# Attention and feed-forward layer: value matmuls taken one head group late, value and output projections in each other's place

## What is computed

```python
qkv = hidden_states @ Wqkv
q, k, v = jnp.split(qkv, 3, axis=-1)
q = rmsnorm(q, q_norm_w)
k = rmsnorm(k, k_norm_w)
# 16 heads of 32 columns
q = rope(q, cos, sin)
k = rope(k, cos, sin)
mask = (q_idx >= k_idx) & (q_idx - k_idx <= WINDOW - 1)   # WINDOW = 256
scores = jnp.einsum('bqhd,bkhd->bhqk', q, k) * scale
scores = jnp.where(mask[None, None, :, :], scores, jnp.float32(-jnp.inf))
probs = jax.nn.softmax(scores, axis=-1)
o = jnp.einsum('bhqk,bkhd->bqhd', probs, v).reshape(b, s, h)
return o @ Wo
# and around it: x = layernorm(x + attention(x))
```

## The kernel before

| Group | projection | turned |
|---|---|---|
| 0 | queries of s + 1 | `spread`, the reciprocal sums of block s - 1 |
| 1 | keys of s + 1 | `x1` of block s - 2 |
| 2 | output of s - 1 | the rotated queries of s + 1 |
| 3 | values of s + 1 | the rotated keys of s + 1 |

## Time and profile before

### The profile page before, as it was taken

One profiled execution on the slowest core, in us unless ns is written; L12 is line 12 of the kernel. 1 busy time (PEld: TensorE's weight loads), 2 busy tenths in 40 slices (PEclk: granted clock), 3 DMA queues, 4 the chain that ended last, 5 costly groups with the idle time before them and its releaser, 6 DMA issues.

```text
span 1096.1 us, 19793 instructions
## 1 busy us (share of the span) xinstructions
PE 1039.7 (95%) x7116; PEld 855.9 (78%) x7116; DVE 766.6 (70%) x1165; ACT 639.4 (58%) x1301; POOL 446.9 (41%) x548
## 2 busy tenths in 40 slices
PE   4899999999999977999999999999999999999995
PEld 3677777777777754887888888888888888887884
DVE  4887777787877763874766677777676777674573
ACT  4566666666666654334566666666766666664353
POOL 4677887777788730001122222222222222221271
PEclk8899999999999986899999999999999999999998
DMA  5111111111111103356798999999999999995562
GB/s 203 32 50 33 32 32 31 32 47 47 31 31 32 31 30 109 119 185 214 229 270 245 242 276 260 262 256 262 252 280 258 256 266 258 264 238 135 157 196 90
DMA packets 121265, 171.88 MB, mean 157 GB/s; under 512 B 10144, under 2 KB 63776, under 8 KB 121088
## 3 DMA queue, kind: packets, MB, share of 16 engines
q1 hardware_dynamic: 112432, 150.16, 43.5%
q0 software_dynamic: 8736, 20.45, 11.5%
HBM read 151.97 MB, written 23.07 MB: 160 GB/s over the span
## 4 chain that ended last, share of the span: by engine, by line
PE 58%; DVE 1%; ACT 1%; issue 0%; DMA 0%; POOL 0%; ACTq 0%; POOLq 0%; DVEq 0%
PE up_ps L1349 4%; PE up_ps L1350 4%; PE up_ps L1351 4%; PE down_ps L1376 4%; PE down_ps L1375 4%; PE gate_ps L1349 4%; PE down_ps L1374 4%; PE gate_ps L1350 4%; PE gate_ps L1351 3%; PE e_up_ps L1400 3%; PE e_up_ps L1401 2%; PE e_up_ps L1402 2%; PE e_gate_ps L1409 2%; PE e_up_ps L1411 2%; PE e_up_ps L1409 2%; PE e_up_ps L1410 2%
## 5 line engine op out<-in xcount | busy, mean ns | idle before, releaser
L897 POOL DMA_INDIRECT sum_dram<-rows,target_i x39 | 62.7, 1608 | 367.0 <-ACT rows L997 367.0
L1223 DVE TENSOR_TENSOR e_lo<-e_raw,e_hi 128x1408 fp32r<-128x1408 f32 x78 | 126.6, 1624 | 47.5 <-ACT e_hi L971 47.5
L971 ACT CAST e_hi<-e_raw 128x1408 fp32r<-128x1408 f32 x78 | 107.5, 1379 | 55.4 <-PE e_up_ps L1411 55.4
L257 POOL TENSOR_TENSOR probT<-probT,masks 128x256 f32<-128x256 f32 x128 | 97.3, 781 | 67.5 <-DVE probT L434 67.4
L317 ACT ACTIVATE prob<-score_ps,nbias 128x256 f32<-128x256 f32 x256 | 119.6, 476 | 8.6 <-DVE nbias L413 8.5
L1228 DVE TENSOR_TENSOR ed_lo<-ed_raw,ed_hi 128x1024 fp32r<-128x1024 f32 x39 | 47.8, 1225 | 71.4 <-ACT ed_hi L979 71.4
L903 POOL DMA_INDIRECT rows<-x_dram,token_i x39 | 52.8, 1354 | 102.3 <-DVE target_i L1192 70.3
L325 ACT COPY probT<-probT_ps 128x512 f32<-128x512 f32 x64 | 37.5, 587 | 94.0 <-PE probT_ps L541 94.0
L413 DVE TENSOR_REDUCE nbias<-score_ps 128x2 f32<-128x512 f32 x128 | 88.5, 691 | 4.4
L507 PE MATMUL proj_ps<-wqkv_lo,xT_hi 128*128 128x512 f32 x180 | 79.3, 441 | 0.0
L541 PE MATMUL probT_ps<-ident,prob 128*128 128x128 f32 x512 | 72.1, 286 | 0.0
(11 more groups left out here) (230 smaller groups left out, 2985.0 us busy)
## 6 DMA issues: line engine op xcount, KB each, us to landing
e_raw<-in_We_gu SPq DMA_DIRECT2D x78, 704.0 KB, 5.8
ed_raw<-in_We_down SPq DMA_DIRECT2D x39, 512.0 KB, 5.3
raw_ring<-in_Ws_gu SPq DMA_DIRECT2D x58, 256.0 KB, 6.2
wd_raw<-in_Ws_down SPq DMA_DIRECT2D x44, 256.0 KB, 6.7
gu_raw<-in_Ws_gu SPq DMA_DIRECT2D x30, 256.0 KB, 6.1
ed_raw<-in_We_down SPq DMA_DIRECT2D x39, 192.0 KB, 6.6
xT_in<-in_xT SPq DMA_DIRECT2D x16, 256.0 KB, 2.8
x_in<-in_x SPq DMA_DIRECT2D x16, 256.0 KB, 3.3
```

The lines of the kernel that those rows point to most:

```text
L257: nc.gpsimd.tensor_tensor(probT[:, heads, 2, :], probT[:, heads, 0, :], own_T.unsqueeze(1).to_broadcast([P, 2, P]), ALU.mult).then_inc(own ...
L971: nc.scalar.copy(e_hi[:, half * HK:(half + 1) * HK, :], raw_half(i, half)).then_inc(e_hi_made, 1)
L1223: nc.vector.tensor_tensor(e_lo[:, part, :], raw_half(i, half), e_hi[:, part, :].bitcast(FP32), ALU.subtract).then_inc(e_lo_made, 1)
```

## The change

It does the following.

- `probT` gets two buffers, taken in turn by n. PE's value part at the end of the group that turned the probabilities of n is now that of n - 1. DVE, ACT and POOL write `probT` for n behind the value part of n - 2 (`pv_mm` at n - 1), and the two copies no longer wait for `own_made`.
- PE projects the values in group 2 and the output in group 3. ACT takes the values out of `proj_ps` in group 2. DVE's `res`, statistics and aggregate stand in group 3, behind `xT_lo`.
- The result of the last value part is there one group later, so DVE's `oT` and `oT_lo` and ACT's `oT_hi` go from group 1 to group 2.
- POOL's two layer norm instructions go from the end of group 3 to the head of the next step's group 0, and DVE's `x1` to group 0, behind the second maximum.
- PE's wait for `res_made` stands before the query projection of the next step; before the output projection it waits for `v_made`.

```diff
-        probT = sb("probT", [P, 4, 3, P])
+        probT = sb("probT", [P, 2, 4, 3, P])
...
                 for pair, copied in ((0, probT_dve), (1, probT_act)):
                     wait(pool, copied, n + 1)
-                    wait(pool, pv_mm, n)
+                    wait(pool, pv_mm, n - 1)
...
+                if g == 0 and has(s - 2):
+                    wait(pool, mv_made, s - 1)
+                    nc.gpsimd.tensor_scalar(rstd[:, 1:2], mv[:, 1:2], 1.0, LN_EPS, ALU.mult, ALU.add).then_inc(ln_var, 1)
+                    wait(pool, ln_var, s - 1)
+                    nc.gpsimd.tensor_tensor(rstd[:, 0:1], rstd[:, 1:2], half[:, :], ALU.pow).then_inc(ln_rstd, 1)
                 if has(n // 4):
                     own_part(n)
...
-                if g == 3 and has(s - 1):
-                    wait(pool, mv_made, s)
...
@@ scalar
                 wait(act, probT_mm, 2 * n + 2)
-                wait(act, pv_mm, n)
-                wait(act, own_made, 2 * n)
+                wait(act, pv_mm, n - 1)
...
-                if g == 1 and has(s - 1):
+                if g == 2 and has(s - 1):
                     wait(act, oT_made, s)
...
-                if g == (3 if s >= 0 else 2) and has(a):
+                if g == 2 and has(a):
                     wait(act, v_mm, a + 1)
@@ vector
                 wait(dve, probT_mm, 2 * n + 1)
-                wait(dve, pv_mm, n)
-                wait(dve, own_made, 2 * n)
+                wait(dve, pv_mm, n - 1)
...
-                if g == 1 and has(s - 1):
+                if g == 2 and has(s - 1):
                     wait(dve, pv_mm, 4 * s)
                     wait(dve, rrep_made, s)
...
+                if g == 0 and has(s - 2):
+                    wait(dve, ln_rstd, s - 1)
+                    wait(dve, x1_stored, 16 * (s - 3))
+                    wait(dve, x1T_mm, s - 3)
+                    nc.vector.tensor_scalar(x1[:, s % 2, :], res[:, :], mv[:, 0:1], rstd[:, 0:1], ALU.subtract, ALU.mult).then_inc(x1_made, 1)
                 if s == 0:
                     split_wo(g)
-                if g == 1 and has(s - 1):
+                if g == 2 and has(s - 1):
                     wait(dve, oT_hi_made, s)
...
+                if g == 3 and has(s + 2):
+                    split_xT(s + 2)
-                if g == 2 and has(s - 1):
+                if g == 3 and has(s - 1):
                     wait(dve, wo_mm, s)
                     wait(dve, x1_made, s - 1)
...
-                if g == 3:
-                    if has(s + 2):
-                        split_xT(s + 2)
-                    if has(s - 1):
-                        wait(dve, ln_rstd, s)
...
@@ tensor
                 if g == 0 and has(a):
                     wait(pe, xT_lo_made, a + 1)
                     wait(pe, v_made, a)
+                    wait(pe, res_made, s - 1)
...
-                if g == 2 and has(s - 1):
+                if g == 2 and has(a):
                     wait(pe, k_sq, min(a + 1, NB))
+                    part, done = (x_hi, x_lo, wqkv_hi, wqkv_lo, 2), v_mm
+                if g == 3 and has(s - 1):
+                    wait(pe, v_made, min(a + 1, NB))
                     wait(pe, oT_lo_made, s)
...
-                if g == (3 if s >= 0 else 2) and has(a):
-                    wait(pe, res_made, s)
-                    part, done = (x_hi, x_lo, wqkv_hi, wqkv_lo, 2), v_mm
...
-                if behind:
-                    values(n)
+                if has((n - 1) // 4):
+                    values(n - 1)
```

More of the change, by code:

```diff
@@ L254, in own_part @@
                     wait(pool, copied, n + 1)
-                    wait(pool, pv_mm, n)
+                    wait(pool, pv_mm, n - 1)
                     heads = slice(2 * pair, 2 * pair + 2)
-                    nc.gpsimd.tensor_tensor(probT[:, heads, 2, :], probT[:, heads, 0, :], own_T.unsqueeze(1).to_broadcast([P, 2, P]), ALU.mult).then_inc(own_made, 1)
+                    nc.gpsimd.tensor_tensor(probT[:, n % 2, heads, 2, :], probT[:, n % 2, heads, 0, :], own_T.unsqueeze(1).to_broadcast([P, 2, P]), ALU.mult).then_inc(own_made, 1)
             def v_difference(s):
@@ L294, in _ @@
                     rotate_sin(pool, nc.gpsimd, a, 1, rot_a[:, :], rot_b[:, :], k_part, k_rot)
-                if g == 3 and has(s - 1):
-                    wait(pool, mv_made, s)
-                    nc.gpsimd.tensor_scalar(rstd[:, 1:2], mv[:, 1:2], 1.0, LN_EPS, ALU.mult, ALU.add).then_inc(ln_var, 1)
-                    wait(pool, ln_var, s)
-                    nc.gpsimd.tensor_tensor(rstd[:, 0:1], rstd[:, 1:2], half[:, :], ALU.pow).then_inc(ln_rstd, 1)
         @block.scalar
@@ L322, in probT_out @@
                 wait(act, probT_mm, 2 * n + 2)
-                wait(act, pv_mm, n)
-                wait(act, own_made, 2 * n)
-                nc.scalar.copy(probT[:, 2:4, 0:2, :], probT_ps[1][:, 0, :].rearrange("p (h w t) -> p h w t", h=2, w=2)).then_inc(probT_act, 1)
+                wait(act, pv_mm, n - 1)
+                nc.scalar.copy(probT[:, n % 2, 2:4, 0:2, :], probT_ps[1][:, 0, :].rearrange("p (h w t) -> p h w t", h=2, w=2)).then_inc(probT_act, 1)
             def split_xT(b):
@@ L431, in probT_out @@
                 wait(dve, probT_mm, 2 * n + 1)
-                wait(dve, pv_mm, n)
-                wait(dve, own_made, 2 * n)
-                nc.vector.tensor_copy(probT[:, 0:2, 0:2, :], probT_ps[0][:, 0, :].rearrange("p (h w t) -> p h w t", h=2, w=2)).then_inc(probT_dve, 1)
+                wait(dve, pv_mm, n - 1)
+                nc.vector.tensor_copy(probT[:, n % 2, 0:2, 0:2, :], probT_ps[0][:, 0, :].rearrange("p (h w t) -> p h w t", h=2, w=2)).then_inc(probT_dve, 1)
             split_xT(0)
@@ L489, in _ @@
                     nc.vector.bn_aggr(mv[:, :], bn6[:, :]).then_inc(mv_made, 1)
-                if g == 3:
-                    if has(s + 2):
-                        split_xT(s + 2)
-                    if has(s - 1):
-                        wait(dve, ln_rstd, s)
-                        wait(dve, x1_stored, 16 * (s - 2))
-                        wait(dve, x1T_mm, s - 2)
-                        nc.vector.tensor_scalar(x1[:, (s - 1) % 2, :], res[:, :], mv[:, 0:1], rstd[:, 0:1], ALU.subtract, ALU.mult).then_inc(x1_made, 1)
         @block.tensor
@@ L557, in values @@
                         last = nc.tensor.matmul(oT_ps[HD * h:HD * h + HD, 0, g * P:(g + 1) * P], v[:, head * HD:(head + 1) * HD],
-                                                probT[:, h, w, :], start=(w == 0), stop=(w == WB - 1))
+                                                probT[:, n % 2, h, w, :], start=(w == 0), stop=(w == WB - 1))
                 last.then_inc(pv_mm, 1)
```

## The result

The changed kernel takes 1106.9 us (median of 4 runs, 1105.83 to 1107.8) against 1095.8 for the kernel before (4 runs, 1093.05 to 1097.83): a ratio of 1.0099, interval 1.0085 to 1.0112. It is **11 us slower**, where 5.5 were forecast on the median. The direction was right and the time lies inside the range, but the change is twice the size. The profiled execution took 1105.83 us, 7.9 more than that of before.

What follows compares the result with a forecast made beforehand. PE was taken to set the pace of the block step, others mattering only where it waits. Terms -5.9 + 8.5 + 6.1 - 0.9 - 2.0 = +5.8 us on the 1095.5 us median gave 1101 us, range 1091 to 1108.

Steps and rivals of the forecast that it cites:

- Values late: Group 1: PE no longer waits for POOL's masked part, 0.45 us saved in steps 2 to 14, -5.9 us.
- DVE's chain: Group 0: residual and statistics delay DVE's probT copy, PE waits 0.65 us in each of 13 steps, +8.5 us.
- POOL's chain: Group 3, key turn: PE waits for POOL's rotated keys, 0.1 us in 7 steps, 0.9 in 6 with copies, +6.1.
- The x1 conflict: Group 0, steps with key copies: x1 on DVE lengthens POOL's work by 0.44 us; without it 2.7 us less.
- The layer norm's pair: Group 0: POOL's two layer norm instructions fit its idle time, zero cost; otherwise some 0.8 us onto the key copies.
- Start: Step 0: the value projection fills group 2, where PE stalls; at most 1.39 us back, -0.9 taken.
- End: Step 15: the output projection fills PE's 2.41 us wait before the values in group 3; -2.0 us taken.
- The base: Whole kernel: the +5.8 us sum was put on the 1095.5 us median; the profiled execution was 2.4 above it.
- only the DVE wait: Rival, group 3: POOL's chain has its slack back, so the 6.1 us go; 1095 us, chance 0.15.
- DVE's chain is hidden: Rival, group 0: DVE does the residual while waiting elsewhere, so the new waits mostly don't come; 1087 us, chance 0.13.
- Weight loads drawn ahead: Rival, before value parts: early release ends 0.1 us idle in 60 places, 6 us back; 1095 us, chance 0.06.
- The clock falls: Rival: new waits lower PE's granted clock; six key steps paying 1.5 us each make 1110 us, chance 0.09.

Runs made afterwards that it cites:

- swap_only: Kernel before with only the exchange of output and value projection, values not late, one buffer; 1106.37 us, ratio 1.0105 to the kernel before.
- stats_late: Changed kernel with statistics behind the second maximum in group 0, x1 and POOL's layer norm pair later too; 1107.35 us, ratio 1.0102 to the kernel before.
- stats_twice: Changed kernel with one more statistics instruction on DVE, its result unused; 1112.38 us, ratio 1.0147 to the kernel before.
- after_again: The changed kernel run once more, unaltered, as the mark for runs beside it; 1105.3 us, ratio 1.008 to the kernel before.
- tail_early: all_three, but in the last blocks statistics, POOL's pair and x1 at the changed kernel's places; 1092.58 us, ratio 0.9968 to the kernel before.
- both: stats_late plus POOL's masked part behind the rotation in groups 1 and 2; 1095.16 us, ratio 1.0008 to the kernel before.
- after: The changed kernel itself, with the whole change, against the kernel before; 1106.9 us, ratio 1.0099.
- all_three: both, with POOL's key copies moved to the head of group 3; 1094.13 us, ratio 0.9992 to the kernel before.
- copies_last: Changed kernel with POOL's key copies moved from group 0 to group 3, ahead of the masked part; 1107.51 us, ratio 1.0101 to the kernel before.
- tail_v_late: tail_early with v_step on POOL moved to group 1, behind the masked part; 1095.76 us, ratio 0.9999 to the kernel before.

## Why the prediction was right in direction and wrong in size

1. *Values late*, -0.45 a step: group 1 became 5.77 to 5.79 us. Its 6.24 before was worked out from 5.80 for each other group; PE's scores in that trace are 6.26 to 6.27 apart. So it is -0.48 a step, -6.2 in all. Right as a size and as a place. It was not worth that in the sum, since POOL took most of it back; the prediction had said so (its "0.65 less the 0.45"), and `swap_only` shows it: the late values save 0.15 or 0.12 a step.
2. *DVE's chain*, 0.65 in group 0: measured 0.66, 13 x 0.66 = +8.6. Right, and `stats_late` and `stats_twice` show the cause from both sides.
3. *POOL's chain*, **the step that failed**: "about 0.1 us of new wait in group 3" was 0.31, so 7 steps cost 2.2 and not 0.7. The slack of 0.33 was taken from POOL's end (216.73) to PE's start (217.06), and the slack after the change was let run down to zero. But PE never starts at POOL's end: the earlier trace rows show 207.41 - 207.27 = 0.14 there, and after the change it is 0.15. The usable slack was 0.33 - 0.15 = 0.18, and 0.18 - 0.48 = -0.30. The DVE term had this hand-over in it (0.05), the POOL term had not. In the steps with copies 0.82 came instead of 0.9, two errors that nearly cancel: the hand-over and the 0.03 of (1) added 0.2, and the chain starts 0.5 late and not 0.8 (230.68, 7.78 us after the step's scores, where 6.62 + 0.66 = 7.28 was due). The x1 conflict took less than the 0.44 set for it: v_step lasts 1.47 against the 1.29 of the kernel before, 0.18 more. The rule of the Trainium skill's "SBUF — State Buffer", section "SBUF: two separate sides", holds here in kind: x1 and POOL's long instructions do lengthen each other.
4. *The layer norm's pair*: nothing, as said. Its warning held in `stats_late`, where the pair stood in the chain and group 2 grew to 6.26 in the copy steps.
5. *Start*, -0.9: -1.0, which is partly luck: the traced start of before was granted 0.91, that of after 0.96, and `after_again` has -1.6. *End*, -2.0: **-1.3**, mis-sized by 0.7. The 2.41 is gone, but in the step behind it PE has a new wait for DVE's copy. The sum allowed 0.4 us (2.4 less 2.0) for all that the late chain costs there:

```profile
416.44 0.66 PE L511 MATMUL probT_ps<-ident,spread 128*128 128x128 f32 x4 [1.11 <-DVE probT L432]
```

   And the last output projection waits 2.28 us for `oT_lo`, where it waited 1.22 before. How the 0.7 divides among these, and what the clock adds, is not shown. `stats_late` and `tail_early` show the end to hang on DVE's residual chain by 4 to 5.5 us.
6. *The base.* The steps sum to +5.8 against +7.9 between the two profiled executions: 1.5 too little for group 3, 0.5 too much for the copies, 0.7 too much for the end, 0.5 in the next phase. The other 3.2 us of the 11.1 lie between profiles and medians: the profiled execution before was 2.1 over its median, that after 1.1 under it. The prediction added its sum to the median as if the profiled execution's 2.4 over it didn't bear on the difference. The runs show what those 3.2 go with: in 50 further executions of the kernel before, those with a mean granted clock of 0.974 to 0.977 took 1095.89 to 1097.63 us, those with 0.982 or 0.983 took 1092.73 to 1094.13, which is some 0.5 us for each 0.001 (an estimate). The profiled execution of before had 0.974, against a median of 0.979; that of after had 0.982, against a median of 0.979 for its eight runs with those of `after_again`. By that estimate the clock of the two traces accounts for the 3.2, and it hid a part of the loss. In which stretch is not settled: the start and the end of the trace of before are the ones at a lower clock than in the changed kernel's two traces, and two places that vary from run to run are shown below.

In short: the two new waits came where they were forecast, and POOL's was mis-sized by 1.0 us in the sum (7.1 for 6.1). Of the 5.6 us between 1101.3 and 1106.9, this makes 1.0 in the middle, the end 0.7 and the next phase 0.5; the most lies in the base.

Of the rivals, *only the DVE wait* fell with group 3's 0.31. *DVE's chain is hidden* did not come by itself, but its mechanism is real: with the statistics and the masked part moved by hand (`both`), the step is 23.16. *Weight loads drawn ahead* fell: the weight loads still idle 21.3 / 59 = 0.36 us before each value part, with the masked part ready more than 5 us before. So what the Trainium skill's "TensorE: Matmul & The Clock Gate", Part 2, says of weight loads pulled ahead of matmuls does not close this gap. *The clock falls* did not come in the middle, where it is granted 1.00.

## What to carry to other kernels

When a change moves work between the groups of a hand-written order, list for each engine what stands ahead of the instruction that PE waits for, and shift all of it, for the waits that go as well as for those that come: a wait removed from the pacing engine runs down the slack of every chain that had hidden behind it. Take the hand-over between engines off each slack before comparing; a slack of 0.33 us with 0.15 of hand-over in it is half gone. And move the work that has gained slack (here the masked part) behind the work that has none, which was worth 7 us, more than the change's own gain.

## What was not expected of the hardware

- **DVE and POOL hold each other up for most of an instruction.** x1 takes 0.54 alone, 0.82 where it meets the end of a POOL instruction, 1.30 and 1.50 where it starts beside `v_step` (1.28). In all three traces (`after`, `stats_late`, `all_three`) it ends 0.28 to 0.29 after the POOL instruction does, as if it had been held until then. The statistics (0.68 to 0.69) are not lengthened beside the masked product. `xT_lo` takes 0.68 alone and 1.02 (`copies_last`) to 1.29 (`both`) beside the masked product, which takes 1.43 alone and 1.88 beside `oT_lo`. So it isn't always POOL that pays, and each move of a piece to a free spot made a new collision (`copies_last`, `tail_v_late`).
- **The hand-over depends on the engine**: 0.14 to 0.15 us from POOL to PE, 0.05 to 0.06 from DVE to PE, in each of the 13 steps of `after`.
- **The clock falls in two places, and the code doesn't tell when.** The first is at the end of step 0, where PE now idles 0.3 (`after`) to 1.9 us (`copies_last`) before its scores. `stats_late` and `stats_twice` do the same up to there, since their edits bear on later groups. PE's timelines, of the first and of the second:

```profile
51.07 0.45 PE L526 MATMUL score_ps<-kT_lo,qT_hi 32*128 32x384 f32 x4 [1.31 <-issue]
...
51.80 1.09 PE L539 MATMUL probT_ps<-ident,prob 128*128 128x128 f32 x8
```

```profile
50.88 0.69 PE L527 MATMUL score_ps<-kT_lo,qT_hi 32*128 32x384 f32 x4 [1.33 <-issue]
...
52.14 1.97 PE L540 MATMUL probT_ps<-ident,prob 128*128 128x128 f32 x8
```

The second runs at the lower of the two levels (1.2 instead of 2.4 GHz, granted 0.50 instead of 1.00), and that group lasts 8.72 instead of 6.09 us. In `after` the low stretch lies just before these scores (0.50 granted in the 2 us ahead of them), and the group lasts 6.24. Seven of the ten experiments last longer there: 7.25 and 7.35 in `both` and `all_three`, 8.3 to 8.7 in `copies_last`, `swap_only`, `stats_twice`, `tail_early` and `tail_v_late`. The other place is the first 30 us of the next phase, whose code is the same in all kernels. The view by stretch, of `after` and of `swap_only`:

```profile
431.81:461.81 30.00, 27.82 (x131) 19.76 (x132) 18.59 (x77) 15.53 (x21) 0.67 (x8) 0.76 0.46 132
```

```profile
438.31:468.31 30.00, 27.88 (x150) 20.68 (x151) 22.27 (x88) 16.01 (x22) 0.68 (x8) 0.91 0.53 149
```

With 0.76 to 0.81 granted there, in ten of the twelve traces, the phase lasts 671 to 672 us; with 0.91 or 0.92, in `swap_only` and `all_three`, it lasts 667. Such steps of 2 and 5 us are of the size of the runs' scatter (`both`: 1092.33 to 1101.08). That these two places are where the open 3.2 us lie is not shown: both single traces of before and after have the long form of the next phase.
